# Row sums of the softmax: two more steps of a unit folded over two key blocks, and two of the folded sums added on GpSimd to the next step's

## The reference

```python
h = layernorm(x) * (1 + ca) + sa
q, k, v = per-head projections of layernorm(h)
q, k = layernorm(rotary(q)), layernorm(rotary(k))
scores = causal(q @ k.T / sqrt(32))
a = softmax(scores) @ v
x = x + ga * (a @ Wo + bo)
h = layernorm(x) * (1 + cb) + sb
x = x + gb * ((silu(h @ Wg.T) * (h @ Wu.T)) @ Wd.T)
```

## Time and profile before

| | us |
|---|---|
| median of three runs | 2279.6 (2278.38 to 2283.41) |
| the profiled execution | 2278.27, its span 2276.5 |

### The profile page before, as it was taken

The page is one execution under the profiler, slowest core; times in us unless marked ns, Lnnn a source line. Parts: engine busy times, 40 slices in busy tenths (PEclk is TensorE's granted clock), DMA queues, the critical chain, the costliest instruction groups (busy, mean ns, idle before and its releaser), DMA issues. The chain is left out here.

```text
span 2276.5 us, 35811 instructions
## 1 busy us (share of the span) xinstructions
PE 2125.2 (93%) x13416; PEld 1661.8 (73%) x13416; DVE 1219.2 (54%) x2843; ACT 806.6 (35%) x1607; POOL 830.2 (36%) x676
## 2 busy tenths in 40 slices
PE   6999996499999999996896999999999999999998
PEld 3777774367777777774685888888888888888887
DVE  5999997577878787884893222222222212222212
ACT  3433332056666666665683111111111111111111
POOL 2677676224443444443304722222222222222221
PEclk9999998589999999998998999999999999999999
DMA  6122222646666767642883412121211212121111
GB/s 241 56 100 103 92 97 102 146 116 162 150 163 149 163 149 164 148 105 83 271 302 126 130 52 73 51 68 56 70 39 51 64 56 70 51 70 56 51 33 56
DMA packets 175601, 243.93 MB, mean 107 GB/s; under 512 B 20604, under 2 KB 99580, under 8 KB 174936
## 3 DMA queue, kind: packets, MB, share of 16 engines
q1 hardware_dynamic: 173176, 235.56, 36.2%
q0 software_dynamic: 1216, 3.16, 0.5%
q10 hardware_dynamic: 1056, 3.15, 0.4%
HBM read 131.69 MB, written 59.26 MB: 84 GB/s over the span
## 5 line engine op out<-in xcount | busy, mean ns | idle before, releaser
L1435 DVE TENSOR_TENSOR f_gu<-f_psU,f_silu 128x512 f32<-128x512 f32 x128 | 88.6, 692 | 706.1 <-PE f_psU L1505 706.1
L1051 ACT ACTIVATE b_probT<-b_psB 128x512 f32<-128x512 f32 (+1 forms) x640 | 315.2, 555 | 139.5 <-PE b_psB L891 139.4
L1391 POOL TENSOR_SCALAR f_wd_hi<-f_wd 128x512 fp32r<-128x512 f32 x128 | 84.1, 657 | 717.8 <-PE f_psD L1488 717.8
L971 DVE TENSOR_REDUCE b_top<-b_psA 128x2 f32<-128x1024 f32 (+2 forms) x320 | 284.5, 902 | 91.0 <-PE b_psA L868 90.9
L1411 ACT ACTIVATE f_silu<-f_psG 128x512 f32<-128x512 f32 x128 | 76.5, 598 | 504.8 <-PE f_psG L1505 504.8
L891 PEld LDWEIGHTS b_psB<-b_stack 98*128 98x128 f32 x1280 | 184.2, 190 | 73.1 <-issue 38.4
L891 PE MATMUL b_psB<-b_stack 98*128 98x256 f32 (+1 forms) x1280 | 218.8, 291 | 6.2 <-ACT b_probT L1051 3.9
L1503 PE MATMUL f_psG<-f_hT_hi,w_hi 128*128 128x512 f32 x512 | 200.2, 391 | 12.4 <-DVE f_hT_lo L1429 12.4
L1406 ACT ACTIVATE f_gu_hi<-f_gu 128x512 fp32r<-128x512 f32 x128 | 80.9, 632 | 364.6 <-DVE f_gu L1435 364.6
L868 PE MATMUL b_psA<-b_stack 96*128 96x512 f32 (+3 forms) x768 | 184.3, 370 | 24.0 <-DMA b_stack<-b_halves 18.7
L1504 PE MATMUL f_psG<-f_hT_hi,w_lo 128*128 128x512 f32 x512 | 199.9, 390 | 0.0
(11 more groups left out here) (179 smaller groups left out, 4014.2 us busy)
## 6 DMA issues: line engine op xcount, KB each, us to landing
b_stack<-b_halves SPq DMA_DIRECT2D x192, 256.0 KB, 4.8
f_wd<-in_wd_t SPq DMA_DIRECT2D x128, 256.0 KB, 2.7
qkv_d<-a_t SPq DMA_DIRECT2D x32, 512.0 KB, 2.7
b_land<-qkv_d SPq DMA_DIRECT2D x32, 512.0 KB, 4.3
a_x<-in_x SPq DMA_DIRECT2D x32, 256.0 KB, 3.3
qkv_d<-a_v SPq DMA_DIRECT2D x32, 256.0 KB, 3.0
b_v<-qkv_d SPq DMA_DIRECT2D x16, 512.0 KB, 6.6
att_d<-b_acc SPq DMA_DIRECT2D x16, 512.0 KB, 3.2
```

Source lines behind the costliest of these rows:

```text
L971: last = dve.tensor_reduce(into, tile[:, :, col:col + whole_blocks * P], AX.X, ALU.max, negate=True)
L1051: act.activation(probT[:, (NW * n + w) % PROBS, j, 0:width], psB[:, i % BANKS, 0:width], ACT.Exp).then_inc(s["expd"], 1)
```

## The change

All six full steps are paired. DVE keeps 3, 6 and 8, POOL has 1, 4 and 7. Behind its pair of step 4, POOL adds to it the pair of step 3, which DVE has made (`MERGED`), and behind that of step 7 the pair of step 6. PE makes no product with ones for steps 3 and 6; those of 4 and 7 cover two steps each. `pairs` has three places instead of two: 0 for POOL's pairs, 1 for steps 3 and 6, 2 for step 8. Counts of semaphores are worked out anew, and the ring of `probT` is released by DVE's pair where a step has no product with ones.

```diff
-    PAIRED = [w for w, (q, g) in enumerate(BLOCKS) if g != q and w != NW - 3]
-    BY_VECTOR = PAIRED[1::2] + PAIRED[4:]
+    PAIRED = [w for w, (q, g) in enumerate(BLOCKS) if g != q]
+    BY_VECTOR = [3, 6, 8]
+    MERGED = {4: 3, 7: 6}
+    PLACE = {1: 0, 3: 1, 4: 0, 6: 1, 7: 0, 8: 2}
+    SUMMING = [w for w in range(len(BLOCKS)) if w not in MERGED.values()]
...
-        pairs = sb("b_pairs", [P, 2, 4, QW])
+        pairs = sb("b_pairs", [P, 3, 4, QW])
...
             def pair(n, w):
-                at = paired_index(n, w)
-                if at >= 2:
-                    before = NW * ((at - 2) // len(PAIRED)) + PAIRED[(at - 2) % len(PAIRED)]
-                    pool.wait_ge(s["summed"], before + 1)
+                before = {1: (n - 1, 7), 4: (n, 1), 7: (n, 4)}[w]
+                at_least(pool, s["summed"], summed_by(*before) if before[0] >= 0 else 0)
+                prob = probT[:, (NW * n + w) % PROBS]
                 for x in range(2):
                     heads = slice(2 * x, 2 * x + 2)
                     pool.wait_ge(s["expd"], 4 * (NW * n + w) + 2 * x + 2)
-                    prob = probT[:, (NW * n + w) % PROBS, heads]
-                    pool.tensor_tensor(pairs[:, at % 2, heads], prob[:, :, 0:QW], prob[:, :, QW:W], ALU.add).then_inc(s["paired"], 1)
+                    pool.tensor_tensor(pairs[:, 0, heads], prob[:, heads, 0:QW], prob[:, heads, QW:W], ALU.add).then_inc(s["paired"], 1)
+                if w in MERGED:
+                    pool.wait_ge(s["paired_v"], paired_v_by(n, MERGED[w]))
+                    for x in range(2):
+                        heads = slice(2 * x, 2 * x + 2)
+                        pool.wait_ge(s["paired"], paired_by(n, w) - 3 + x)
+                        pool.tensor_tensor(pairs[:, 0, heads], pairs[:, 0, heads], pairs[:, 1, heads], ALU.add).then_inc(s["paired"], 1)
...
+                if summing and w in MERGED.values():
+                    return
                 if summing and w in PAIRED:
...
                     for j in range(4):
+                        if j % 2 == 0 and w in BY_VECTOR:
+                            pe.wait_ge(s["paired_v"], paired_v_by(n, w) - 1 + j // 2)
+                        elif j % 2 == 0:
+                            pe.wait_ge(s["paired"], paired_by(n, w) - 1 + j // 2)
+                        mm = pe.matmul(out[j * HD:(j + 1) * HD], ones[:], pairs[:, PLACE[w], j],
                                        start=False, stop=False, skip_group_check=True)
...
             def pair(n, w):
+                if w == 8:
+                    at_least(dve, s["summed"], summed_by(n - 1, 8) if n else 0)
+                else:
+                    at_least(dve, s["paired"], paired_by(n, 4) if w == 6 else paired_by(n - 1, 7) if n else 0)
...
                 if j == 0:
-                    at_least(act, s["summed"], NW * n + w - 2)
                     at_least(act, s["weighed"], NW * n + w - 2)
+                    if NW * n + w >= PROBS:
+                        last = divmod(NW * n + w - PROBS, NW)
+                        if last[1] in MERGED.values():
+                            act.wait_ge(s["paired_v"], paired_v_by(*last))
+                        else:
+                            act.wait_ge(s["summed"], summed_by(*last))
```

More of the change, by code:

```diff
@@ L627, in attention_stage, with summed_by, paired_by, paired_v_by @@
     DIAGONAL = [w for w, (q, g) in enumerate(BLOCKS) if g == q]
-    PAIRED = [w for w, (q, g) in enumerate(BLOCKS) if g != q and w != NW - 3]
-    BY_VECTOR = PAIRED[1::2] + PAIRED[4:]
-    def paired_index(n, w):
-        return len(PAIRED) * n + PAIRED.index(w)
+    PAIRED = [w for w, (q, g) in enumerate(BLOCKS) if g != q]
[3 more added lines that the diff above has]
+    SUMMING = [w for w in range(len(BLOCKS)) if w not in MERGED.values()]
+    def summed_by(n, w):
+        return len(SUMMING) * n + sum(1 for x in SUMMING if x <= w)
+    def paired_by(n, w):
+        return sum(4 if x in MERGED else 2 for x in PAIRED if x not in BY_VECTOR) * n + sum(4 if x in MERGED else 2 for x in PAIRED if x not in BY_VECTOR and x <= w)
+    def paired_v_by(n, w):
+        return 2 * (len(BY_VECTOR) * n + sum(1 for x in BY_VECTOR if x <= w))
     def cut_at(k):
@@ L1000, in pair @@
                     dve.wait_ge(s["expd"], 4 * (NW * n + w) + 2 * x + 2)
-                    prob = probT[:, (NW * n + w) % PROBS, heads]
-                    dve.tensor_tensor(pairs[:, at % 2, heads], prob[:, :, 0:QW], prob[:, :, QW:W], ALU.add).then_inc(s["paired_v"], 1)
+                    dve.tensor_tensor(pairs[:, PLACE[w], heads], prob[:, heads, 0:QW], prob[:, heads, QW:W], ALU.add).then_inc(s["paired_v"], 1)
             def finish(q):
@@ L1058, in take @@
             def take(n, q):
-                act.wait_ge(s["summed"], NW * n + DIAGONAL[q] + 1)
+                act.wait_ge(s["summed"], summed_by(n, DIAGONAL[q]))
                 at_least(act, s["scaled"], n - 1)
```

## The result

The changed kernel takes 2342.6 us (median of four runs, 2340.19 to 2344.34), against 2281.5 for the kernel before in the same runs: a ratio of 1.0268, interval 1.0249 to 1.0286, so 61 us slower. The direction was forecast, the size was not: 2320 with a range up to 2334. The profiled execution has a span of 2340.8 us, and its mean granted clock is 0.953 instead of 0.970.

The account below looks back on a forecast made before the run. PE was taken as the bound, without a gap. Waits of 27.0, 11.7 and 2.5 us, net of removed work, gave +41.2 us on the profiled 2278.3, so 2320 us; own range 2310 to 2333, 8 in 10 from 2284 to 2334.

Parts of the forecast that it names:

- The bound and the direction: Whole kernel: PE is the bound without a gap, each wait costs its full time; slower, given 0.89.
- The removed work: PE's sums of steps 3 and 6 and half of step 7's: 0.43 us each, 1.30 us a unit saved.
- Step 4: PE's sum waits about 1 us for POOL's merges; the turn of step 6 starts 0.55 us later.
- gather: DVE's four instructions at step 7 take turns with POOL's additions, end 2 us late; turn of step 9 1.25 us later.
- The row of the first stage: Sign for full waits: a 128x32 DVE operation ended 0.04 us behind a POOL addition, at 203.06 after starting at 202.23.
- Step 8 and normalise: DVE's late pair 8 meets POOL's normalise and delays the third item's maxima: 0.9 us in 13 units.
- The sum of the waits: Over attention: 27.0 us for 15 units, 11.7 for step 8 and normalise, 2.5 for the last unit: +41.2 us.
- The clock: Rival: PE's 2.1 us idle stretch in each unit brings about a microsecond at half clock, 2340 to 2360 us; chance 0.06.
- one stretch of the output projection: Sign against the clock falling: PE waits of up to 2.5 us there at a granted clock of 1.00.

Follow-up runs that it names:

- all_paired: The changed kernel with nothing merged: all six steps paired, steps 3, 4, 6 and 7 each with their own sum; 2278.4 us against 2281.35 for the kernel before.
- merge4: As all_paired, but with the first merge alone, the pair of step 3 added to that of step 4; 2288.0 us, ratio to the kernel before 1.0030.
- experiment 6: The changed kernel with POOL's merge of step 7 held back until gather is through; 2302.95 us, ratio to the kernel before 1.0103.
- filler: The changed kernel with 16 products with zeros, 1.73 us of PE work, in front of each turn_peaks; 2324.5 us, ratio to the kernel before 1.0190.
- experiments 1 and 2: The changed kernel with 1.73 us (filler) or 0.86 us of PE products with zeros in front of each turn_peaks; 2324.5 and 2325.5 us.
- all_paired_swap: As all_paired, with DVE's pair of step 8 moved behind the maxima of its turn's first score item; 2303.5 us, ratio to the kernel before 1.0099.
- merge4_later: As merge4, with the sum of step 4 moved on PE by a turn, in front of the sum of step 5; 2272.6 us against 2280.0, ratio 0.9964.

## Why the prediction was right and wrong

**The bound and the direction: right.** PE had no gap, and everything given to it as a wait came back as time. The removed work was sized right: 0.44 us a unit in all_paired against 0.43.

**Step 4: right mechanism, a little smaller.** Forecast 0.55 us later, measured 0.45 (37.90 against 37.45 us in most units of merge4 and all_paired). In the changed kernel's unit the merges start at 573.06 and end at 575.58; the turn of step 6 starts at 576.19, 0.61 us behind, where 0.69 was reckoned.

**gather: right, by the row it was read from.** Forecast: L984, L986 and the cast or L991 wait for one POOL instruction each, gather 2 us late, PE idle 2.1 us, the turn of step 9 1.25 us later. Measured: 0.26, 1.21, 1.19 and 0.19 us for the four, so the middle two were held for a whole instruction and the others hardly; PE idle 1.96 to 2.00 us, and from the turn of step 6 to that of step 9 12.85 us (576.19 to 589.04) instead of 11.48, 1.37 later. The row of the first stage, a 128x32 operation that ended 0.04 us behind a POOL addition, said this of the small operations, and experiment 6 shows it by taking the meeting away. By the GPSIMD Engine Reference of the Trainium skill, Specifications, GpSimd shares its SBUF interfaces with VectorE. The trace agrees and gives the price here: a full wait for the running instruction, 1.21 us where it was 0.19.

**Step 8 and normalise: right, a little smaller.** At full clock (filler) a unit is 2.54 us longer than before; less 0.45 for step 4 and 1.37 for gather that leaves 0.7, where 0.9 was forecast (the two for gather and step 4 are from one unit, so the rest is an estimate to a tenth or two). **The sum of the waits** was forecast at 41.2 us and is 43 (2324.5 - 2281.35). Attention from its first to its last product is 702.8 us in filler against 661.0.

**The clock: the step that failed.** In the sum it stands at nothing. The prediction named it as a rival, with the idle stretch of 2.1 us, priced it at 20 to 40 us, and gave it 0.06, on the strength of one stretch of the output projection, with PE waits of up to 2.5 us at a clock of 1.00. That row holds other work: there PE was idle 9 of 119 us and had long products of 512 columns around each wait. It says that a pause of this length need not bring a fall, not that it can't. Here it came behind 12 of 15 and cost 18 us, shown by experiments 1 and 2, which change hardly more than what PE does in the pause. That the rival's 2340 to 2360 holds the measured time is in part luck: it was priced for a microsecond or so at half clock, which is half a microsecond of work, some 8 us in 15 units. The falls were 3.4 or 6.8 us long, and part of their cost fell into waits. Rows from other work could not carry a chance as low as 0.06; with one in four the range would have reached beyond 2342.

**Not settled.** Why the clock fell behind 12 of 15 pauses of 1.97 us and behind only 4 of 14 of 1.72 us. The length of one pause does not decide it alone. In filler a wait of 1.63 us at `prepare` brought no fall, while in all_paired_swap one of 3.4 us came behind waits of 0.88 and 0.20 us, and another in the last unit of merge4_later behind a wait of 1.31 us. The wait and the window behind it, in this order:

```profile
754.63 1.06 PE L873 MATMUL b_psA<-b_ident,b_land 128*128 128x128 f32 x8 [1.63 <-DVE b_corner L1001]
```
```profile
753.00:760.00 7.00, 5.37 (x65) 4.10 (x65) 5.28 (x21) 3.34 (x7) 3.39 (x3) 1.00 0.27 77
```
```profile
862.91 0.62 PE L933 MATMUL b_psOL<-b_pairs,b_ones 128*32 128x256 f32 x4 [0.88 <-DVE b_pairs L1023]
```
```profile
864.50:867.80 3.30, 3.30 (x26) 2.39 (x30) 2.24 (x2) 1.24 (x3) 0.93 (x1) 0.50 0.00 0
```
```profile
1047.25 0.86 PE L942 MATMUL b_psOL<-b_probT,b_v 128*32 128x256 f32 x16 [1.31 <-POOL b_probT L824]
```
```profile
1048.30:1051.60 3.30, 3.30 (x31) 2.20 (x20) 0.97 (x2) 1.44 (x3) 0.00 (x0) 0.50 0.02 5
```

Why 0.23 us a unit are missing in merge4_later: there PE's weight loads wait for the exponents in more turns (25.9 us in 67 places, against 18.0 in 48 in merge4), which fits a bound by ACT one turn after the removed sum, but no run takes that wait away. (gather's first instruction is held there too, 633 ns on average, but PE does not wait at turn_peaks in the thirteen units.) A kernel with merge 7 alone was not tried.

## What to carry to other kernels

Work moved from a bound engine to an idle one is paid in latency at the place where the result is asked for: find out when the idle engine is done, on the timeline, and put the consumer behind that. The same merge cost 9.6 us with its product in one place and gained some 5 with it one turn later (0.9964 against 0.9987 of the kernel before). Before putting work on GpSimd, look at what VectorE does in that same stretch; in a chain of four short VectorE instructions two were held for one GpSimd instruction each, and made the unit 1.37 us longer, against 0.45 us for the merge of step 4. And when a forecast contains a pause of TensorE of a microsecond or two in every round, the clock belongs in the sum.

## What the runs showed of the hardware that I had not expected

- In front of turn_peaks, TensorE's clock fell to the 1.2 GHz level at 12 of 15 pauses of 1.97 us, at 4 of 14 of 1.72 us, and at none of 1.15 us or of 0.3 us. Elsewhere two falls came behind waits of 0.9 and 1.3 us. The falls behind turn_peaks began between 0.2 us before the end of the pause and 2.2 us behind it, mostly in the middle of work, and lasted 3.4 or 6.8 us.
- Work without any use, put into the pause, made the kernel 18 us faster.
- The cost of a fall is in part hidden by the next wait: PE's wait at `prepare` was 0.9 us in all with the falls and 8.5 us without them.
- A 128x32 combination of two SBUF inputs on VectorE, and also a 128x32 cast, waited for the running GpSimd addition to end, though each is short: 0.19 us became 1.2.
